# Expert choice in three parts with lists of 512 tokens, two of them worked out beside the experts' products, and the expert bias inside the activation

## The chip, the cores and the metric

The kernel runs on one core of one Trainium2 chip. The metric is the device time of one execution in microseconds (us), and the median of three runs stands for the kernel. A core has five engines with instruction queues of their own: TensorE (PE in the profile), VectorE (DVE), ScalarE (ACT), GpSimd (POOL) and SyncE (SP), which wait for each other on semaphores.

## The reference

Two transformer blocks run one after the other over x of 4 x 1024 tokens of 256 numbers. The change is in the second half of the first block, a mixture of 48 experts in which the experts choose tokens:

```
xf = h.reshape(-1, D)                      # T = 4096 tokens, D = 256
cap = int(1.5 * T / E)                     # E = 48 experts, cap = 128
logits = xf @ Wr.T
vals, idx = top_k(logits.T, cap)           # each expert takes its best 128 tokens
w = softmax(vals)
xg = xf[idx]
h = gelu(einsum('ecd,esdm->ecsm', xg, W1) + b1)      # S = 4 slices, M = 256
y = einsum('ecsm,esmk->ecsk', h, W2) + b2            # K = 64
out = zeros.at[idx].add(y * w)
```

Before it stands an attention of its own, behind it a second block (a Performer with an elu network, and another network); neither is touched.

## The kernel before

The program is a chain of blocks with a barrier between them: `front`, three blocks of `expert_choice`, then `performer` and `networks`. The blocks of `expert_choice` are these.

The first normalises the tokens in 8 groups of 512, writes them to `h_dram`, and puts the logits into `logits`, where rows 0 to 47 hold the first 2048 tokens for each of the 48 experts and rows 64 to 111 the other 2048.

The second block finds the best tokens. VectorE runs 16 rounds over rows of 2048 numbers: `max` gives the 8 largest, `max_index` their places, `match_replace` wipes them out (L825 to L828). Then the two halves of each expert are merged by a few small products and operations, which leaves `index` and `weight` (one column of 128 for each expert). Beside the rounds, SyncE loads the weights of the first 8 experts, and TensorE and ScalarE fold the key and query weights of the second block and work out its constants (`fold_ps`, L899 to L919).

The third block is the loop over the 48 experts. Each expert needs these steps, by the names in the code:

- `gather(e)` on GpSimd: copies the indices to `slot`, then an indirect DMA brings the 128 rows of the expert from `h_dram` to `xg`;
- `turn(e)` on TensorE transposes them, `x_copy(e)` on ScalarE brings them to `xT`;
- `up(e)` on TensorE: 16 products into `h_ps`; VectorE adds the bias (`pre`, L1053), ScalarE applies gelu in one operation of 128 x 1024 (L1027);
- `down(e)` on TensorE: 8 products into `y_ps`; VectorE adds b2 (`biased_y`, L1064);
- `weigh(e)` on ScalarE multiplies by the weights into `y` (L1032), and the scatter of expert e on GpSimd adds the rows to a sum in DRAM by an indirect DMA (L999).

Every engine works its queue in the order that the code gives. TensorE goes up(e + 1), turn(e + 2), down(e). ScalarE goes gelu(e + 1), weigh(e), x_copy(e + 3). GpSimd goes scatter(e), gather(e + LEAD), where `LEAD` is 6, so that six gathers are issued ahead of the first scatter. SyncE loads expert e + 8 once `biased_y` of expert e is there.

Of the kernel before, what the change touches and what calls it, by code (L numbers as in the profile page):

```python
# [12 lines left out]
ALU = mybir.AluOpType  # L13
# [575 lines left out]
TOP = 8  # L589

def expert_choice(nc, mk, g, a):

    HALF = T // 2
    LOW = 64
    ROWS = LOW + E
    with ExitStack() as ctx:
# [6 lines left out]
        weight = t.sb("weight", [P, E])  # L604
        h_dram = nc.dram_tensor("h_dram", (T, D), F32, kind="Internal").ap()
# [10 lines left out]
        with ExitStack() as c2:  # L616
            r = Maker(nc, c2)
            logits = r.sb("logits", [ROWS, HALF])

            with ExitStack() as c3:  # L620
                t = Maker(nc, c3)
                z, hg = t.sb("z", [P, 2, G, D]), t.sb("hg", [P, 2, G, D])
                hT = t.sb("hT", [P, 2, KD, GT])
                wrT = t.sb("wrT", [P, KD, E])
                st, mv, var, rstd, shift = (t.sb("st1", [P, G, 6]), t.sb("mv1", [P, 2, G, 2]), t.sb("var1", [P, 2, G]), t.sb("rstd1", [P, 2, G]),
                                            t.sb("shift1", [P, 2, G]))
                tp, lp, back = t.ps("tp1", [P, 2, KD, GT]), t.ps("lp1", [P, 2, GT]), t.ps("back1", [P, G, D])
                own, blank, var_ready, rstd_ready, shift_ready = (mk.sem("ec_dve"), mk.sem("ec_blank"), mk.sem("ec_var"), mk.sem("ec_rstd"),
                                                                  mk.sem("ec_shift"))
                z_ready, turned, hT_ready, back_done, h_ready = (mk.sem("ec_z"), mk.sem("ec_turned"), mk.sem("ec_hT"), mk.sem("ec_back"),  # L630
                                                                 mk.sem("ec_h"))
                logits_done, logits_out, wrT_done, wrT_copied = (mk.sem("ec_logits"), mk.sem("ec_logits_out"), mk.sem("ec_wrT"),
                                                                 mk.sem("ec_wrT_copied"))
                h_out = [mk.sem("ec_h_out0"), mk.sem("ec_h_out1")]
                part = lambda n: slice(LOW * (n // (NG // 2)), LOW * (n // (NG // 2)) + E)
                with nc.Block() as block:
                    @block.sync
                    def _(sp):
                        for n in range(NG):
                            sp.wait_ge(h_ready, n + 1)  # L640
                            sp.dma_start(h_dram[n * GT:(n + 1) * GT, :].rearrange("(t p) d -> p t d", p=P), hg[:, n % 2]).then_inc(h_out[n % 2], 16)
                        for k in range(2):
                            sp.wait_ge(h_out[k], 16 * (NG // 2))

                    @block.gpsimd
                    def _(pool):
                        pool.memset(logits[32:64, :], LOWEST).then_inc(blank, 1)
                        pool.wait_ge(blank, 1)
                        for n in range(NG):
                            pool.wait_ge(var_ready, n + 1)  # L650
                            if n >= 2:
                                pool.wait_ge(shift_ready, n - 1)
                            rsqrt_rows(pool, rstd[:, n % 2], var[:, n % 2], g.minus_half, G, rstd_ready)

                    @block.vector
                    def _(dve):
                        v = Steps(dve, own)

                        def update(n):
                            for j in range(n * G, (n + 1) * G):  # L660
                                row = g.x[:, j, :]
                                v.mark(dve.scalar_tensor_tensor(row, g.gated[:, n // 2, :], g.tok[:, j:j + 1], row, ALU.mult, ALU.add))
                            v.sync()

                        def statistics(n):
                            if n >= 2:
                                dve.wait_ge(z_ready, n - 1)
                            layer_norm_stats(v, g.spare, st, mv[:, n % 2], var[:, n % 2], G, lambda j: g.x[:, n * G + j, :], LN_EPS, var_ready)

                        def shift_of(n):  # L670
                            dve.wait_ge(rstd_ready, n + 1)
                            dve.scalar_tensor_tensor(shift[:, n % 2], mv[:, n % 2, :, 0], -1.0, rstd[:, n % 2], ALU.mult, ALU.mult).then_inc(shift_ready, 1)

                        def logits_copy(n):
                            dve.wait_ge(logits_done, n + 1)
                            if n == 0:
                                dve.wait_ge(blank, 1)
                            dve.tensor_copy(logits[part(n), n % (NG // 2) * GT:(n % (NG // 2) + 1) * GT], lp[part(n), n % 2, :]).then_inc(logits_out, 1)
# [1714 lines left out]
```

## Time and profile before

| | |
|---|---|
| median of 3 runs | 1726.31 us (1724.62 to 1728.32) |
| profiled execution, its own time | 1728.49 us |
| its span, first to last instruction | 1726.7 us |
| busy: PE, DVE, ACT, POOL | 1495.2, 1171.5, 642.8, 526.5 us |
| block that finds the tokens | about 150 to 270 us |
| loop over the experts | about 270 to 562 us |

### The profile page before, as it was taken

What the parts mean: (1) busy time and instruction counts of PE and PEld (TensorE: products, weight loads), DVE (VectorE), ACT (ScalarE), POOL (GpSimd) and SP (SyncE); (2) the same over time, 40 slices, a digit from 0 to 9 for tenths busy, and PEclk for the clock granted to TensorE, in tenths of its full rate; (3) what the DMA queues carried; (4) which work ended last, traced back from release to release, by engine and by line L of the source; (5) the groups of instructions that cost most, each with busy time, mean ns of one, the idle gap of its engine ahead of it and who ended that gap; (6) DMA issues with size and microseconds to landing.
All of it is one profiled execution on the core that took longest, in us unless ns stands there. A gap on an engine that the chain in (4) does not pass through costs nothing. (4 is left out here: it accounts for less than half of the span.)

```text
span 1726.7 us, 22918 instructions
## 1 busy us (share of the span) xinstructions
PE 1495.2 (87%) x8460; PEld 1248.3 (72%) x8460; DVE 1171.5 (68%) x1867; ACT 642.8 (37%) x947; POOL 526.5 (30%) x511
## 2 busy tenths in 40 slices
PE   8874236999998399999997999999976999989997
PEld 6442236999998266666655788888865888878887
DVE  6576992222222668877737878787856987798886
ACT  1044102333333122222222333333326776766774
POOL 2410003555554012222224200000003555546666
PEclk7788657999999599999998999999997999999999
DMA  5516903999993301112113000000012100000001
GB/s 195 220 37 235 320 6 98 296 292 297 297 291 58 123 25 37 37 37 62 36 49 110 0 25 25 25 25 25 13 52 98 50 25 14 1 1 25 13 25 37
DMA packets 127835, 157.16 MB, mean 91 GB/s; under 512 B 13952, under 2 KB 95992, under 8 KB 126720
## 3 DMA queue, kind: packets, MB, share of 16 engines
q1 hardware_dynamic: 115952, 138.12, 24.6%
q0 software_dynamic: 9216, 12.59, 3.6%
q10 hardware_dynamic: 2576, 5.26, 0.8%
q8 instruction: 54, 0.88, 0.2%
q14 instruction: 37, 0.30, 0.1%
HBM read 122.35 MB, written 33.60 MB: 90 GB/s over the span
## 5 line engine op out<-in xcount | busy, mean ns | idle before, releaser
L2031 POOL TENSOR_TENSOR ff_hid_lo<-ff_hid,ff_hid_hi 128x512 fp32r<-128x512 f32 x128 | 176.0, 1376 | 161.1 <-ACT ff_hid_hi L1940 161.1
L1082 PE MATMUL h_ps<-xT,w 128*128 128x128 f32 x1536 | 192.9, 284 | 1.0 <-ACT xT L1023 1.0
L1082 PEld LDWEIGHTS h_ps<-xT,w 128*128 128x128 f32 x1536 | 186.3, 197 | 1.6 <-issue 0.9
L1053 DVE TENSOR_TENSOR pre<-h_ps,b1T 128x1024 f32<-128x1024 f32 x48 | 58.8, 1225 | 176.4 <-PE h_ps L1082 176.4
L2315 PE MATMUL ff_down<-ff_w_hi,ff_hid_hi 128*128 128x256 f32 x512 | 147.7, 288 | 4.1 <-POOL ff_hid_lo L2031 3.6
L2317 PE MATMUL ff_down<-ff_w_hi,ff_hid_lo 128*128 128x256 f32 x512 | 146.4, 286 | 0.0
L2316 PE MATMUL ff_down<-ff_w_lo,ff_hid_hi 128*128 128x256 f32 x512 | 146.2, 286 | 0.0
L116 POOL TENSOR_TENSOR ff_rstd<-ff_var,minus_half 128x4 f32<-128x4 f32 x24 | 25.5, 1061 | 358.9 <-DVE ff_var L111 356.6
L1117 PE MATMUL k_ring<-w_hi,hT_hi 128*128 128x512 f32 x256 | 118.7, 464 | 9.5 <-DVE hT_lo L1277 6.4
L1458 PE MATMUL k_acc<-wide_rows,hk 128*128 128x512 f32 x256 | 119.7, 599 | 4.3 <-ACT wide_rows L1402 4.3
L1117 PE MATMUL q_ring<-w_hi,hT_hi 128*128 128x512 f32 x256 | 109.8, 429 | 9.8 <-PEq L99 6.8
L1747 PE MATMUL q_out_ps<-kv_sums,wide_rows 128*128 128x256 f32 x512 | 115.5, 379 | 0.0
L2301 PE MATMUL ff_ring<-ff_rowsT_hi,ff_w_hi 128*128 128x512 f32 x256 | 103.0, 402 | 8.4 <-DVE ff_rowsT_lo L2089 3.6
L2315 PEld LDWEIGHTS ff_down<-ff_w_hi,ff_hid_hi 128*128 128x128 f32 x512 | 99.1, 194 | 10.6 <-POOL ff_hid_lo L2031 5.0
L1747 PEld LDWEIGHTS q_out_ps<-kv_sums,wide_rows 128*128 128x128 f32 x512 | 96.3, 190 | 13.2
L2302 PE MATMUL ff_ring<-ff_rowsT_lo,ff_w_hi 128*128 128x512 f32 x256 | 102.4, 400 | 0.0
L2316 PEld LDWEIGHTS ff_down<-ff_w_lo,ff_hid_hi 128*128 128x128 f32 x512 | 99.3, 194 | 4.2
L1119 PE MATMUL k_ring<-w_hi,hT_lo 128*128 128x512 f32 x256 | 102.2, 399 | 0.0
L1118 PE MATMUL k_ring<-w_lo,hT_hi 128*128 128x512 f32 x256 | 101.8, 398 | 0.0
L1119 PE MATMUL q_ring<-w_hi,hT_lo 128*128 128x512 f32 x256 | 101.7, 397 | 0.0
L1118 PE MATMUL q_ring<-w_lo,hT_hi 128*128 128x512 f32 x256 | 101.6, 397 | 0.0
L1393 ACT ACTIVATE k_squares<-k_ring 128x1024 f32<-128x1024 f32 x32 | 32.8, 1025 | 182.3 <-PE k_ring L1119 182.3
(374 smaller groups left out, 3537.4 us busy)
## 6 DMA issues: line engine op xcount, KB each, us to landing
w<-in_L_ffn_W_dram SPq DMA_DIRECT2D x48, 1024.0 KB, 5.8
w<-in_L_ffn_W_dram SPq DMA_DIRECT2D x48, 256.0 KB, 6.1
expert_sum_dram<-f_zero SPq DMA_DIRECT2D x8, 1024.0 KB, 14.9
b_rows<-in_L_ffn_b_dram SPq DMA_DIRECT2D x48, 128.0 KB, 8.8
x<-in_L_attn_x_dram SPq DMA_DIRECT2D x4, 1024.0 KB, 12.4
h_dram<-hg SPq DMA_DIRECT2D x8, 512.0 KB, 2.9
hk<-expert_sum_dram SPq DMA_DIRECT2D x8, 512.0 KB, 4.4
hT_hi<-expert_sum_dram SPq DMA_DIRECT2D x8, 512.0 KB, 5.2
```

The source lines that it names most:

```text
L1082: last = pe.matmul(h_ps[:, q % 2, s * KD + c, :], w1[:, q, s, k, c::KD], xT[:, q % 2, k, :], start=(k == 0), stop=(k == KD - 1))
L1117: pe.matmul(out, x[0], w[0][:, cols], start=start, stop=False)
L1118: pe.matmul(out, x[0], w[1][:, cols], start=False, stop=False)
L1119: return pe.matmul(out, x[1], w[0][:, cols], start=False, stop=stop)
L1458: last = pe.matmul(acc[:, k, cols], hk[:, n % KV_RING, j, k * P:(k + 1) * P], dash[:, n % 2, j, cols], start=(j == 0), stop=(j == G - 1))
L1747: last = pe.matmul(out_ps[:, i % 2, 0:D], qnT[:, i % 2, c, :], kv_out(i // TB)[:, c, :], start=(c == 0), stop=(c == CH - 1))
L2031: pool.tensor_tensor(hid_lo[:, m % PARTS, :], hid[:, m % WHOLES, :], hid_hi[:, m % PARTS, :].bitcast(F32), ALU.subtract).then_inc(part_low, 1)
L2301: pe.matmul(slot(u), high[:, d, cols], x[:, n % 2, d, :], start=(d == 0), stop=False)
L2302: pe.matmul(slot(u), high[:, d, cols], x_low[:, n % 2, d, :], start=False, stop=False)
L2315: pe.matmul(into, hid_hi[:, m % PARTS, tile], high[:, c, :], start=(c == 0 and j % 2 == 0), stop=False)
L2316: pe.matmul(into, hid_hi[:, m % PARTS, tile], low[:, c, :], start=False, stop=False)
L2317: last = pe.matmul(into, hid_lo[:, m % PARTS, tile], high[:, c, :], start=False, stop=(c == CF - 1 and j % 2 == 1))
```

## The change

The experts are dealt with in three parts of 16 (`PHASES`, `EP`). Each part has its own tile of 128 lists, 8 for each of its 16 experts, and each list holds the logits of 512 tokens. SyncE spreads the logits to the lists with three small DMAs for each group. A part needs 16 rounds over rows of 512, and then a merge of the 8 lists of each expert: the lists are sent by TensorE to the 16 experts' rows, sorted down level by level with pairs of max and min until the smallest and the largest of the best 128 are known, each list counts how many of its numbers are above the edge, and the lists' heads are moved to their place by seven steps of doubling length (`move`), once for the indices and once for the weights.

The second and third blocks become one. Part 0 is worked out ahead of the loop. The rounds and the merges of parts 1 and 2 stand in VectorE's queue in slots behind `add(e)`, and TensorE's and ScalarE's pieces of them in slots of the loop. The folds and constants of the second block now use the memory of `h_ps` and of two of the experts' weight buffers, ahead of `up(0)`. The bias of the hidden layer is no longer added by VectorE: gelu reads `h_ps` directly in 8 operations of 128 x 128 with the bias as an operand. `down(e)` also waits for `biased_y` of expert e - 1. `LEAD` is 3: the indices of part 1 come out in the slot of expert 12, and expert 16 is gathered behind the scatter of expert 13. The loops are written out.

```diff
 
 RING = 8
 TOP = 8
+PHASES = 3
+EP = E // PHASES
+LISTS = P // EP
+AHEAD, STARTS, ROUND_SLOTS, COUNTS_AT = 6, (0, 0, 13), (0, 5, 8), (0, 9, 25)
 
...
+                @block.sync
+                def _(sp):
+                    def spread(n):
+                        sp.wait_ge(logits_out, n + 1)
+                        for i in range(PHASES):
+                            sp.dma_start(lists[n * EP:(n + 1) * EP, i, :], stage[i * EP:(i + 1) * EP, n % 2, :]).then_inc(lists_in[n % 2], 16)
+
+                    for n in range(NG):
+                        sp.wait_ge(h_ready, n + 1)
+                        sp.dma_start(h_dram[n * GT:(n + 1) * GT, :].rearrange("(t p) d -> p t d", p=P), hg[:, n % 2]).then_inc(h_out[n % 2], 16)
+                        if n >= 2:
+                            spread(n - 2)
+                    spread(NG - 2)
+                    spread(NG - 1)
...
-            XG, LEAD = 8, 6
+            XG, LEAD = 8, 3
...
+                    def gather(e):
+                        if e % EP == 0:
+                            pool.wait_ge(indexed, e // EP + 1)
+                        if e >= XG:
+                            pool.wait_ge(turned, e - XG + 1)
+                        pool.tensor_copy(slot[:, e % XG], index[:, e:e + 1]).then_inc(slot_set, 1)
                         pool.wait_ge(slot_set, e + 1)
-                        carry_wait(n)
...
+                    def scatter(e):
+                        pool.wait_ge(y_ready, e + 1 + 2)
+                        carry()
+                        pool.indirect_dma_start(out=sums[e % 2], out_offset=bass.IndirectOffsetOnAxis(ap=slot[:, e % XG], axis=0),
+                                                in_=y[:, e % 2, :], in_offset=None, compute_op=ALU.add).then_inc(added[e % 2], 16)
...
+                    for e in range(E):
+                        scatter(e)
+                        if e + LEAD < E:
+                            gather(e + LEAD)
+                        if e:
+                            pool.wait_ge(added[(e - 1) % 2], 16 * ((e + 1) // 2))
+                            pool.sem_inc(y_free, 1)
...
+                    def gelu(e):
+                        act.wait_ge(up_done, e + 1)
+                        for s in range(S):
+                            for c in range(KD):
+                                last = act.activation(act_h[:, e % 2, s * KD + c, :], h_ps[:, e % 2, s * KD + c, :], ACT.Gelu,
+                                                      bias=b1T[:, e * S + s, c:c + 1])
+                        last.then_inc(gelu_done, 1)
...
+                    for e in range(E):
+                        if e + 1 < E:
+                            gelu(e + 1)
+                        weigh(e)
+                        if e + 3 < E:
+                            x_copy(e + 3)
+                        if e == COUNTS_AT[1]:
+                            exps(1)
+                        if e == COUNTS_AT[2]:
+                            exps(2)
...
+                    def rounds(p, first, count):
+                        for n in range(first, first + count):
+                            cols = slice(n * TOP, (n + 1) * TOP)
+                            v(dve.max(top[:, cols], lists[:, p, :]))
+                            v(dve.max_index(at[:, cols], top[:, cols], lists[:, p, :]))
+                            if n < CAP // TOP - 1:
+                                v(dve.match_replace(lists[:, p, :], top[:, cols], lists[:, p, :], LOWEST))
+
+                    def listed(p):
+                        dve.sem_inc(found, 1)
+                        v(dve.tensor_copy(at_f[:], at[:]))
+
...
+                    def sort_steps(lists_left, first, count):
+
+                        for i in range(first, first + count):
+                            j = P >> (i + 1)
+                            of, to = (order[:, (i + x) % 2, 0:lists_left, :].rearrange("e q (b i j) -> e (q b) i j", i=2, j=j) for x in range(2))
+                            v.mark(dve.tensor_tensor(to[:, :, 0, :], of[:, :, 0, :], of[:, :, 1, :], ALU.max))
+                            v.mark(dve.tensor_tensor(to[:, :, 1, :], of[:, :, 0, :], of[:, :, 1, :], ALU.min))
+                            v.sync()
+
+                    def second_level():
...
+                    def move(lists, first, count):
+
+                        for i in range(first, first + count):
+                            of, to, step = lists[:, i % 2, :], lists[:, (i + 1) % 2, :], 1 << i
+                            v(dve.tensor_scalar(to, of, bits[:, 1, i:i + 1], None, ALU.mult))
+                            v(dve.scalar_tensor_tensor(to[:, step:], of[:, 0:P - step], bits[:, 0, i:i + 1], to[:, step:], ALU.mult, ALU.add))
+
...
+                    def add(e):
                         dve.wait_ge(down_done, e + 1)
                         dve.wait_ge(y_ready, e + 1)
-                        dve.tensor_tensor(biased_y[:, q % 2, :], y_ps[:, q % 2, 0:D], b2_rows[:, q, :], ALU.add).then_inc(y_biased, 1)
...
+                    rounds(0, 0, CAP // TOP)
+                    listed(0)
+                    turn_back(0)
+                    first_level(0)
+                    sort_steps(4, 0, 7)
+                    second_level()
+                    sort_steps(2, 0, 7)
+                    last_level()
+                    counts(0)
+                    placed(0)
+                    move(moved, 0, 7)
+                    dve.sem_inc(shifted, 1)
+                    weights_in(0)
+                    indices(0)
+                    move(moved_w, 0, 7)
+                    dve.sem_inc(valued, 1)
+                    rounds(1, 0, AHEAD)
+                    weights(0)
+                    for e in range(E):
+                        add(e)
+                        for p in range(1, PHASES):
+                            k = e - STARTS[p]
+                            if 0 <= k < ROUND_SLOTS[p]:
+                                rounds(p, CAP // TOP - 2 * (ROUND_SLOTS[p] - k), 2)
+                            if k == ROUND_SLOTS[p] - 1:
+                                listed(p)
+                            if e == COUNTS_AT[p] - 4:
...
+                            if e == COUNTS_AT[p] - 1:
+                                sort_steps(2, 0, 7)
+                                last_level()
+                            if e == COUNTS_AT[p]:
+                                counts(p)
+                            if e == COUNTS_AT[p] + 1:
+                                placed(p)
+                                move(moved, 0, 3)
+                            if e == COUNTS_AT[p] + 2:
+                                move(moved, 3, 4)
+                                dve.sem_inc(shifted, 1)
+                            if e == COUNTS_AT[p] + 3:
...
+                    def down(e):
                         pe.wait_ge(gelu_done, e + 1)
+                        if e:
+                            pe.wait_ge(y_biased, e)
...
+                        for k in range(KD):
+                            last = pe.matmul(fold_ps[:, 1024 + c * B:1024 + (c + 1) * B], w_raw[1][:, k, c * P:(c + 1) * P], g.shift_col[:, k, :],
+                                             start=(k == 0), stop=(k == KD - 1))
+                    last.then_inc(wave_consts, 1)
+                    join_weights(0)
+                    turn(0)
+                    pe.wait_ge(consts_out, 1)
+                    up(0)
+                    turn(1)
+                    for e in range(E):
+                        if e + 1 < E:
+                            up(e + 1)
+                        if e + 2 < E:
+                            turn(e + 2)
+                        for p in range(1, PHASES):
...
+                        for p in range(1, PHASES):
+                            if e == COUNTS_AT[p]:
+                                send_edge(p)
         mk.clear_signals()
```

GpSimd's queue where the loop begins, before (L984 with L980 and L987 is a gather, L980 with L999 a scatter; the number of gathers ahead of the first scatter is what to look at):

```order
L984 COPY slot<-index 128x1
L980 TENSOR_TENSOR pool_spare<-minus_half 128x1
L987 DMA xg<-h_dram,slot 128x256
L984 COPY slot<-index 128x1
L980 TENSOR_TENSOR pool_spare<-minus_half 128x1
L987 DMA xg<-h_dram,slot 128x256
L980 TENSOR_TENSOR pool_spare<-minus_half 128x1
L999 DMA expert_sum0_dram<-y,slot 4096x256
L984 COPY slot<-index 128x1
L980 TENSOR_TENSOR pool_spare<-minus_half 128x1
L987 DMA xg<-h_dram,slot 128x256
```

These are the gathers of experts 4 and 5 (four more stand above them), the scatter of expert 0, and the gather of expert 6. The same place in the changed kernel, from the table that the merge needs on:

```order
L882 AFFINE_SELECT before<-same 128x128
L858 COPY slot<-index 128x1
L850 TENSOR_TENSOR pool_spare<-minus_half 128x1
L861 DMA xg<-h_dram,slot 128x256
L858 COPY slot<-index 128x1
L850 TENSOR_TENSOR pool_spare<-minus_half 128x1
L861 DMA xg<-h_dram,slot 128x256
L858 COPY slot<-index 128x1
L850 TENSOR_TENSOR pool_spare<-minus_half 128x1
L861 DMA xg<-h_dram,slot 128x256
L850 TENSOR_TENSOR pool_spare<-minus_half 128x1
L872 DMA expert_sum0_dram<-y,slot 4096x256
```

Only experts 0 to 2 are gathered ahead of the scatter of expert 0; the gather of expert 3 has moved behind it.

TensorE's queue at the start of the loop in the changed kernel (L1182 is `turn`, L1191 `up`, L1202 `down`; the order of the three is that of before):

```order
L1182 MATMUL x_ps<-ident,xg 128x128 x2
L1191 MATMUL h_ps<-xT,w1 128x128 x16
L1182 MATMUL x_ps<-ident,xg 128x128 x2
L1191 MATMUL h_ps<-xT,w1 128x128 x16
L1182 MATMUL x_ps<-ident,xg 128x128 x2
L1202 MATMUL y_ps<-w2,act_h 128x64 x8
L1191 MATMUL h_ps<-xT,w1 128x128 x16
L1182 MATMUL x_ps<-ident,xg 128x128 x2
L1202 MATMUL y_ps<-w2,act_h 128x64 x8
```

These are turn(0), up(0), turn(1), up(1), turn(2), down(0), up(2), turn(3), down(1). Nothing has moved here, so turn(3) stands ahead of down(1).

ScalarE's queue in the loop of the changed kernel (L902 is `x_copy`, L908 gelu, L915 `weigh`):

```order
L902 ACTIVATE xT<-x_ps 128x256
L908 ACTIVATE act_h<-h_ps,b1T 128x128 x8
L915 ACTIVATE y<-biased_y,weight 128x256
L902 ACTIVATE xT<-x_ps 128x256
L908 ACTIVATE act_h<-h_ps,b1T 128x128 x8
```

In the place of one operation of 128 x 1024 from `pre` there are now eight of 128 x 128 from `h_ps`, ahead of each `weigh`.

## Rows read from the trace of the kernel before

**Rows 1.** The page: 40 slices of the span, PE busy and its granted clock.

```profile
PE   8874236999998399999997999999976999989997
PEclk7788657999999599999998999999997999999999
```

**Rows 2.** Windows: window length, each engine's busy us (instructions), PEclk, DMA share, GB/s.

```profile
148.00:270.00 122.00, 35.38 (x189) 32.49 (x189) 113.77 (x94) 8.73 (x10) 0.61 (x3) 0.62 0.53 181
280.00:530.00 250.00, 249.53 (x2159) 249.34 (x2157) 71.61 (x86) 84.97 (x130) 135.04 (x211) 1.00 0.96 275
```

**Rows 3.** Timeline of VectorE, the rounds: start, us, engine, line, operation.

```profile
150.20 2.29 DVE L825 MAX8 top<-logits 112x8 f32<-112x2048 f32 x1 [1.90 <-PEq L636]
...
157.31 2.29 DVE L825 MAX8 top<-logits 112x8 f32<-112x2048 f32 x1
...
259.35 2.29 DVE L826 FIND_INDEX8 at<-top,logits 112x8 uint32<-112x2048 f32 x1
```

**Rows 4.** Groups by line and form, 262 to 290 us: two widths of VectorE.

```profile
L1053 DVE TENSOR_TENSOR pre<-h_ps,b1T 128x1024 f32<-128x1024 f32 x2 | 2.5, 1225 | 15.4 <-PE h_ps L1082 15.4
...
L1064 DVE TENSOR_TENSOR biased_y<-y_ps,b_rows 128x256 f32<-128x256 f32 x1 | 0.4, 425 | 0.6 <-PE y_ps L1091 0.6
```

**Rows 5.** Timeline of TensorE, the constants of the second block.

```profile
215.03 6.96 PE L912 MATMUL fold_ps<-ff_ln_col,w_raw 128*128 128x1 f32 x32 [15.37 <-DMA w_turned<-in_L_attn_W_dram]
221.85 5.08 PE L915 MATMUL fold_ps<-w_turned,ones 128*128 128x256 f32 x16
```

**Rows 6.** Timeline of all engines from the first index to the first gather in the loop.

```profile
270.40 0.19 POOL L984 COPY slot<-index 128x1 uint32<-128x1 uint32 x1 [119.38 <-POOLq L790]
...
274.53 0.70 PE L1073 MATMUL x_ps<-ident,xg 128*128 128x128 f32 x2 [5.64 <-DMA xg<-h_dram,slot]
...
275.27 0.38 ACT L1023 ACTIVATE xT<-x_ps 128x256 f32<-128x256 f32 x1 [7.09 <-PE x_ps L1073]
275.80 5.57 PE L1082 MATMUL h_ps<-xT,w 128*128 128x128 f32 x32 [0.56 <-ACT xT L1023]
...
282.02 1.28 ACT L1027 ACT_TABLE_LOAD   x1
...
288.09 0.42 DVE L1064 TENSOR_TENSOR biased_y<-y_ps,b_rows 128x256 f32<-128x256 f32 x1 [0.60 <-PE y_ps L1091]
288.65 0.51 ACT L1032 ACTIVATE y<-biased_y,weight 128x256 f32<-128x256 f32 x1
...
289.59 1.65 POOL L999 DMA_INDIRECT expert_sum_dram<-y,slot  x1 [0.16 <-POOL pool_spare L980]
...
291.86 1.03 POOL L987 DMA_INDIRECT xg<-h_dram,slot  x1
```

**Rows 7.** Timeline of the loop in its steady state, TensorE and ScalarE of one expert.

```profile
303.27 0.39 PE L1073 MATMUL x_ps<-ident,xg 128*128 128x128 f32 x2
303.50 1.90 PE L1091 MATMUL y_ps<-w,act_h 128*128 128x64 f32 x16
303.70 0.38 ACT L1023 ACTIVATE xT<-x_ps 128x256 f32<-128x256 f32 x1 [2.99 <-PE x_ps L1073]
```

**Rows 8.** Tile xg, issue to landing: the gather at 291.86, at 528.69, all 48.

```profile
DMA to landing us min/median/max: 5.1/5.1/5.1
...
DMA to landing us min/median/max: 2.8/2.8/2.8
...
DMA to landing us min/median/max: 2.8/5.5/7.3
```

**Rows 9.** Timeline: four normalising operations of ScalarE with two operand columns.

```profile
139.82 2.07 ACT L699 ACTIVATE z<-x,shift,rstd 128x256 f32<-128x256 f32 x4
```

**Rows 10.** Timeline of GpSimd where no weights are loaded, and the last scatter.

```profile
526.46 1.60 POOL L999 DMA_INDIRECT expert_sum_dram<-y,slot  x1
...
528.69 1.01 POOL L987 DMA_INDIRECT xg<-h_dram,slot  x1
...
558.26 1.56 POOL L999 DMA_INDIRECT expert_sum_dram<-y,slot  x1 [0.15 <-issue]
```

More of the change, by code:

```diff
@@ L1047, in _, with exps @@
-                    bodies(act, body)
+                        act.activation(y[:, e % 2, :], biased_y[:, e % 2, :], ACT.Copy, scale=weight[:, e:e + 1]).then_inc(y_ready, 1)
+                    def exps(p):
+                        act.wait_ge(edge_ready, p + 1)
+                        act.activation(ex[:], top[:], ACT.Exp, bias=edge[:, 1:2]).then_inc(top_exp, 1)
+                    for k in range(2):
+                        act.dma_start(proj2[:, k, :], a["L1_attn_proj"]).then_inc(proj_in, 16)
@@ new lines, in _ @@
+                    for i, name in enumerate(("Wk", "Wq")):
+                        act.dma_start(w_raw[i], a[f"L1_attn_{name}"].rearrange("(k p) h d -> p k (h d)", p=P)).then_inc(raw_in[i], 16)
+                    act.wait_ge(fold_turned, 1)
+                    act.wait_ge(blank, 1)
+                    for i in range(2):
+                        rows = slice(i * DH, (i + 1) * DH)
+                        last = act.activation(features[rows, i * MF:(i + 1) * MF], fold_ps[rows, 0:MF], ACT.Copy, scale=DN)
@@ L1057, in _ @@
[L1057 to L1061 removed]
+                    v = Steps(dve, own)
+                    def rounds(p, first, count):
[5 more added lines that the diff above has]
+                                v(dve.match_replace(lists[:, p, :], top[:, cols], lists[:, p, :], LOWEST))
@@ new lines, in first_level @@
+                    def first_level(p):
+                        sent = pick_ps[0:EP].rearrange("e h (w i n) -> e h w i n", w=2, i=2)
+                        pair, copy = (order[:, i].rearrange("e (h w) n -> e h w n", w=2) for i in range(2))
+                        dve.wait_ge(lists_sent, p + 1)
+                        v(dve.tensor_copy(copy, sent[:, :, :, 0, :]))
+                        v.mark(dve.tensor_tensor(pair[:, :, 0, :], sent[:, :, 0, 1, :], copy[:, :, 0, :], ALU.max))
+                        v.mark(dve.tensor_tensor(pair[:, :, 1, :], sent[:, :, 1, 1, :], copy[:, :, 1, :], ALU.min))
+                        v.sync()
@@ new lines, in _ @@
+                    for c in range(CF):
+                        last = pe.matmul(fold_ps[:, 512:512 + D], g.ones[:], w_turned[:, c, :], start=(c == 0), stop=(c == CF - 1))
+                    last.then_inc(elu_consts, 1)
+                    send_edge(0)
+                    rank(0)
+                    join_indices(0)
+                    pe.wait_ge(wave_w_in, 16)
+                    for c in range(CF):
+                        for k in range(KD):
+                            last = pe.matmul(fold_ps[:, 1024 + c * B:1024 + (c + 1) * B], w_raw[1][:, k, c * P:(c + 1) * P], g.shift_col[:, k, :],
+                                             start=(k == 0), stop=(k == KD - 1))
```

757 lines of the change are left out of this document (374 added, 383 removed).

## The prediction, written before the changed kernel had run

> **What bounds the kernel now.** I read the page's slices first: TensorE is busy nearly throughout, with a hole in slices 4 to 7 in which its granted clock falls too [rows 1]. The windows then tell two stretches apart [rows 2]. From 148 to 270 us VectorE is busy for 113.8 of 122 us and TensorE for 35.4 at a clock of 0.62: the rounds are the bound. From 280 to 530 us TensorE is busy for 249.5 of 250 us at a clock of 1.00, though the DMA engines are busy for 96% as well: the loop is bound by TensorE. One expert takes 50 products as the records count them, and 2159 in 250 us make 5.79 us for each expert. The timeline shows what starts the loop: the first index is copied at 270.40, its rows have come at 274.53 for turn(0), the first scatter is issued at 289.59 [rows 6], the last at 558.26 [rows 10].
>
> **The rounds.** One takes 157.31 - 150.20 = 7.11 us, and all end at 259.35 + 2.29 = 261.64 [rows 3]. VectorE takes 1225 ns for 1024 columns and 425 for 256 [rows 4], so 1.042 ns a column. Three operations with 1536 columns less save 4.80 us: a round of 512 is 2.31 us, and 16 less one `match_replace` (0.7 us) are 36.3 us instead of 111.4. The lists must land first: the last logits are copied shortly before VectorE's next work at 150.20, behind them stand three small DMAs, and a small transfer takes at least 2.8 us here [rows 8], so I start the rounds at 152.4. They end at 188.7.
>
> **The merge, now longer.** By the same two widths a width of 128 costs 0.29 us, 256 costs 0.43, 512 costs 0.69. A hand-over to TensorE and back is 0.75 us (turn at 274.53, copy at 275.27) and a product at the low clock 0.35 us (16 in 5.57) [rows 6]. So: first turn and two copies 1.4; eight products 3.0; first level 1.6; seven steps of two operations of 256 with their waits 6.3; second level 0.6; seven steps of width 128 4.4; last level 0.9. This puts the edge at 207. It goes out behind TensorE's constants of the second block, which take 6.96 + 5.08 us once two weight matrices have landed [rows 5]. They can be loaded only when both folds are done, about 187, and take about 10 us, so TensorE gets free at about 209.5. Then: hand-over 0.8, counts 1.3, hand-over 0.8, some twelve small operations 3.0, fourteen of width 128 4.2, hand-over 0.8, three small ones 0.8. The indices are there at 221.5. The first slot copy to turn(0) is 4.1 us as before, and turn(0) waits another 0.9 for the product that joins the weights: 226.6 instead of 274.5, 47.9 us earlier. The uncertain part is the load behind the folds; with it 10 us late the gain is 38.
>
> **Up to the first y.** Before, 274.53 to 289.16 (288.65 + 0.51), 14.6 us [rows 6]. VectorE now has fourteen moves of the weights (4.2 us) and six rounds of part 1 (13.9 us) there, beside the first two `up`: it is free at 240.4, and y(0) ends at about 241.3. No further cost.
>
> **The loop: a chain that did not exist.** This is the large term. TensorE's order is up(e + 1), turn(e + 2), down(e). With a lead of 3, the rows for turn(e + 3) are asked for behind the scatter of e, which needs y of e, so down(e). And turn(e + 3) stands ahead of down(e + 1). So each expert's down waits for a whole way round: down, add, weigh, scatter, gather, turn. Before, the lead of 6 put four experts into one such way round, and 5.79 x 4 us covered it. From the landing of rows G(e + 2) the way is:
>
> - turn starts 0.04 later; x_copy 0.43 after turn begins at the high clock [rows 7], 0.74 at the low one [rows 6]; x_copy itself 0.38 and 0.04 to the next;
> - gelu(e + 1) stands in ScalarE's queue ahead of weigh(e), now eight operations. Four of width 256 with operand columns took 2.07 us, with 0.5 us between starts [rows 9]; of width 128 I take 0.36 each, 2.9 us. Bounds: 0.29 and 0.41, 2.3 to 3.3. TensorE's turn, down (1.90) and VectorE's add end earlier at the high clock, and together with it at the low one, so ScalarE sets the time;
> - weigh 0.51 + 0.05, then 0.43 to the scatter's issue (289.16 to 289.59) [rows 6];
> - scatter issued to gather issued 2.27 us (289.59 to 291.86), gather to landing 5.1 us where a fresh load of weights is under way [rows 6, 8]: 7.3 together. Bounds: 2.23 + 2.8 = 5.1 without loads [rows 8, 10], 2.3 + 7.3 = 9.6 at the worst under full load [rows 8]. I take 7.3, as the load of expert e + 8 is issued some 2 us ahead of the scatter each time, but no backlog is left from the last.
>
> The sum is 12.1 us at the high clock, 12.4 at the low one, and I take 12.3. TensorE is then idle for half of each round, and this kernel's trace shows its clock low where it has such gaps: 0.62 at 35.4 busy us of 122 [rows 2]. The Trainium skill, "TensorE: Matmul & The Clock Gate", section on HAM oscillation, says that a loop of short bursts between waits for DMAs can begin each burst at the low clock. The trace of before has no such loop; by this rule the whole sum would be 5 us above mine, at 12.4 a round.
>
> Rows 3 to 47 come this way, so there are 44 rounds from G(3) to G(47): 541 us. G(3) is at 241.3 + 0.43 + 7.3 = 249.0. The exponentials of parts 1 and 2 need another table and gelu's back: two loads of 1.28 us and the operation, 2.9 us, twice [rows 6], on ScalarE and so in the chain: 5.8. After G(47) stand down(45), up(47), down(46), gelu(47), down(47), add and weigh: 13 us. The last scatter is then issued at 809 instead of 558.3: 250.7 us later. Everything behind it is as before.
>
> **What costs nothing.** Rounds and merges of parts 1 and 2 are at most 5.5 us of VectorE in a slot, two rounds (4.6) and an add. In a slot of 12.3 us they are hidden; in a slot of 5.79 they would just fit. The bias that VectorE drops (1.2 us) was not on a path. The wait of down(e) for add(e - 1) is over long before. The loads of experts 6 and 7, now behind the constants, have over 40 us.
>
> **Sum.** 1726.7 - 47.9 + 298.6 (the loop's part of the 250.7) = 1977.4 of span, 1.8 more as a run. The profiled execution of before was 2.2 above the median, so I predict 1977 us, 14.5% slower.
>
> **Rivals.**
> 1. The same chain with queues that are nearly idle at each scatter: 5.1 in the place of 7.3 gives 10.1 a round, 97 us less: 1880. For it speaks that only 1.4 MB is moved in each round of 12 us; against it, the load starts just ahead of the scatter, and the very first scatter of before met just that and took the 7.3. The Trainium skill, "DMA: Bandwidth & Descriptors", on the anatomy of a DMA, gives about 2.0 us fixed and a small part by size; my estimate from that page is 4.5 us for the pair and 9.5 a round, a time of 1854. The trace of before is above that everywhere [rows 8]. Chance 0.13.
> 2. The chain with worse transfers or a GpSimd held up beside VectorE's rounds: 9.6 in the place of 7.3 gives 14.6 and 2078. Under full load the median gather took 5.5 [rows 8], which alone adds only 18 us. Chance 0.10.
> 3. The gathers are hidden after all, and the loop goes on at TensorE's 5.79. Then only the 47.9 us at its head count: 1679, faster. It decides from a round of 5.79 + 47.9 / 44 = 6.9 us downward. The least sum of the rows is 0.04 + 0.43 + 0.42 + 2.3 + 0.56 + 0.43 + 5.1 = 9.3, so the chain would have to be misread. Chance 0.03.
> 4. VectorE falls behind: with 5.5 us in a slot that is never the longest part. No time of its own; 0.01.
>
> **How the numbers follow.** The forecast, a chain at 11.0 to 13.6 us, has 0.73, and its own range is 1920 to 2035. The range 1872 to 2045 takes in the first rival and the lighter half of the second. A measurement of this kernel tells 0.2% from no change. Faster by more than that is the third rival, 0.03; no case ends within 0.2%, 0.01; slower 0.96.
>
> **What would show it.** In the changed trace: rounds of 2.3 us on VectorE ending near 189; turn(0) near 227; TensorE waiting ahead of `x_ps` for the DMA of `xg` for about 6 us at every expert from the third or fourth on, some 250 us in sum, which before happened once (5.64 us, rows 6); 12.3 us from one scatter to the next; a granted clock well under 1.00 in the loop; the last scatter near 809. The prediction is wrong if TensorE never waits there, or if scatter and gather together take other than 5 to 10 us.

## The result, and the profile after

The changed kernel takes 1973.6 us (median of 4 runs, 1967.0 to 1978.0) against 1725.5: 1.144 times as long, 95% interval 1.141 to 1.147. The profiled execution took 1967.02 us with a span of 1965.3. The prediction was 1977.

The page of the changed kernel, its span, TensorE's slices and the DMA engines' (slices are 49 us wide here):

```profile
span 1965.3 us, 23238 instructions
...
PE   8774576677777777389999978999999599998998
...
PEclk7886577777877778699999989999999799999999
DMA  5438444444444542301111040000000310000000
```

Where the loop of before stood as a row of nines for over 200 us [rows 1], there are some eleven slices with TensorE mostly at 60 to 80% and its clock at 0.7 to 0.8, and the DMA engines are down to 40 to 50%. No engine is full. That is how a chain looks, in which each engine waits for the one before it.

Windows of the changed kernel: the loop where weights are loaded, and its last part, where none are (columns as in [rows 2]):

```profile
250.00:500.00 250.00, 178.88 (x1041) 173.66 (x1040) 86.28 (x237) 62.62 (x206) 65.48 (x100) 0.75 0.48 137
...
745.00:790.00 45.00, 36.01 (x255) 35.05 (x255) 2.12 (x5) 14.43 (x50) 15.59 (x25) 0.87 0.18 30
```

1041 products in 250 us are about half of what [rows 2] had in a stretch as long. The waits in the loop, 240 to 800 us:

```profile
POOL pool_spare L850 <- ACT y L915: 391.3, 48, 16.5
...
PE x_ps L1182 <- DMA xg<-h_dram,slot: 146.7, 45, 5.6
...
ACT y L915 <- DVE biased_y L1082: 44.5, 36, 3.0
```

TensorE waits for gathered rows at 45 of 48 experts; before, the trace had this wait at the first one alone [rows 6]. The last row is one that the prediction did not have: ScalarE, with its eight gelu operations done, waits for VectorE's add.

The timeline of one way round, from behind one `turn` to the next:

```profile
399.90 3.65 PE L1202 MATMUL y_ps<-w,act_h 128*128 128x64 f32 x16
400.14 2.17 ACT L908 ACTIVATE act_h<-h_ps,b1T 128x128 f32<-128x128 f32 x8
403.35 6.34 PE L1191 MATMUL h_ps<-xT,w 128*128 128x128 f32 x32
403.60 0.42 DVE L1082 TENSOR_TENSOR biased_y<-y_ps,b_rows 128x256 f32<-128x256 f32 x1 [9.82 <-PE y_ps L1202]
...
404.05 0.51 ACT L915 ACTIVATE y<-biased_y,weight 128x256 f32<-128x256 f32 x1 [1.75 <-DVE biased_y L1082]
...
405.03 1.60 POOL L872 DMA_INDIRECT expert_sum_dram<-y,slot  x1 [0.15 <-POOL pool_spare L850]
...
407.45 1.01 POOL L861 DMA_INDIRECT xg<-h_dram,slot  x1
...
412.48 0.70 PE L1182 MATMUL x_ps<-ident,xg 128*128 128x128 f32 x2 [2.79 <-DMA xg<-h_dram,slot]
412.97 3.51 PE L1202 MATMUL y_ps<-w,act_h 128*128 128x64 f32 x16
```

Read it downward: `down` ends, VectorE adds, ScalarE weighs, GpSimd scatters, GpSimd gathers, and only 5.0 us after that can TensorE run the next `turn` and the next `down`. The `up` that stands between hides most of the wait, but not the chain.

The first gather of the loop (expert 3) is issued at 257.18 and the last (expert 47) at 783.42: 44 rounds, 11.96 us each. Up to the gather at 735.89 a round took 12.3 us (478.7 us for 39), behind it, with no more loads, 9.5 (47.5 for 5). Taken apart, the means of the rounds beside loads are 2.29 us from the issue of a scatter to that of the gather behind it, 4.75 from there to the turn, and 5.22 from the turn to the next scatter; in the rounds without loads they are 2.22, 2.81 and 4.1.

The landing times of `xg`, the gather at 407.45, the gathers from 738 us on, and all 48 (as [rows 8]):

```profile
DMA to landing us min/median/max: 5.0/5.0/5.0
...
DMA to landing us min/median/max: 2.7/2.8/2.8
...
DMA to landing us min/median/max: 2.7/4.7/5.1
```

The head of the loop, first VectorE, then TensorE:

```profile
153.10 0.69 DVE L972 MAX8 top<-lists 128x8 f32<-128x512 f32 x1
...
155.41 0.69 DVE L972 MAX8 top<-lists 128x8 f32<-128x512 f32 x1
...
205.60 0.27 DVE L1016 TENSOR_REDUCE edge_row<-order 16x1 f32<-16x128 f32 x1
222.30 0.16 DVE L1022 COPY edge<-pick_ps 128x1 f32<-128x1 f32 x1 [16.44 <-PE pick_ps L1161]
...
232.16 0.17 DVE L1071 CAST index<-pick_ps 128x16 uint32<-128x16 f32 x1
```

```profile
208.91 6.96 PE L1232 MATMUL h_ps<-ff_ln_col,w 128*128 128x1 f32 x32 [14.97 <-DMA w<-in_L_attn_W_dram]
215.72 6.23 PE L1235 MATMUL h_ps<-w_turned,ones 128*128 128x256 f32 x16
221.88 0.38 PE L1161 MATMUL pick_ps<-edge_row,same 16*128 16x2 f32 x2
...
231.89 6.97 PE L1243 MATMUL h_ps<-ff_shift_col,w 128*128 128x4 f32 x32
...
239.57 0.67 PE L1182 MATMUL x_ps<-ident,xg 128*128 128x128 f32 x2
```

A round of `max`, `max_index` and `match_replace` takes 2.31 us. VectorE has the edge of part 0 (the bound that tells the best 128 of each expert from the rest) ready at 205.9 and then waits 16.4 us for it to come back from TensorE, as the edge's product stands in TensorE's queue behind the constants, whose weights land only at 208.8. A second batch of constants, 6.97 us at 231.89, then stands ahead of turn(0), which comes at 239.57: 35 us earlier than before [rows 6], and 7.1 us after the first copy of an index (232.46) where before it was 4.1.

### The profile page after: what moved, and what is told of

Same layout as the page of the kernel before. It is cut to its first block and busy times, and to the rows that moved or that the text cites. A ratio compares the mean times of both kernels' runs of the same rounds, so it can differ in the third digit from the quotient of the medians.

```text
span 1965.3 us, 23238 instructions
## 1 busy us (share of the span) xinstructions
PE 1627.7 (83%) x8535; PEld 1371.2 (70%) x8535; DVE 1176.3 (60%) x2242; ACT 697.1 (35%) x1289; POOL 529.4 (27%) x512
## 5 line engine op out<-in xcount | busy, mean ns | idle before, releaser
L1082 DVE TENSOR_TENSOR biased_y<-y_ps,b_rows 128x256 f32<-128x256 f32 x48 | 20.4, 425 | 413.3 <-PE y_ps L1202 300.0
L1191 PE MATMUL h_ps<-xT,w 128*128 128x128 f32 x1536 | 252.6, 340 | 1.1 <-ACT xT L902 1.1
L1191 PEld LDWEIGHTS h_ps<-xT,w 128*128 128x128 f32 x1536 | 247.5, 253 | 1.7 <-issue 1.7
L1182 PE MATMUL x_ps<-ident,xg 128*128 128x128 f32 x96 | 26.8, 367 | 146.7 <-DMA xg<-h_dram,slot 146.7
L902 ACT ACTIVATE xT<-x_ps 128x256 f32<-128x256 f32 x48 | 18.4, 383 | 362.2 <-PE x_ps L1182 362.2
L1202 PE MATMUL y_ps<-w,act_h 128*128 128x64 f32 x768 | 138.1, 357 | 0.6 <-ACT act_h L908 0.6
L1202 PEld LDWEIGHTS y_ps<-w,act_h 128*128 128x128 f32 x768 | 135.5, 273 | 1.1 <-ACT act_h L908 0.7
L850 POOL TENSOR_TENSOR pool_spare<-minus_half 128x1 f32<-128x1 f32 x96 | 20.1, 209 | 395.3 <-ACT y L915 391.3
L1182 PEld LDWEIGHTS x_ps<-ident,xg 128*128 128x128 f32 x96 | 15.2, 207 | 155.3 <-DMA xg<-h_dram,slot 155.3
L2479 PEld LDWEIGHTS ff_down<-ff_w_hi,ff_hid_hi 128*128 128x128 f32 x512 | 99.2, 194 | 10.6 <-POOL ff_hid_lo L2195 5.0
L908 ACT ACTIVATE act_h<-h_ps,b1T 128x128 f32<-128x128 f32 x384 | 103.9, 390 | 2.8 <-PE h_ps L1191 2.7
## 6 DMA issues: line engine op xcount, KB each, us to landing
x<-in_L_attn_x_dram SPq DMA_DIRECT2D x4, 1024.0 KB, 12.3
```

Of the source, the lines that this page charges most:

```text
L908: last = act.activation(act_h[:, e % 2, s * KD + c, :], h_ps[:, e % 2, s * KD + c, :], ACT.Gelu, bias=b1T[:, e * S + s, c:c + 1])
L1191: last = pe.matmul(h_ps[:, e % 2, s * KD + c, :], w1[:, e % RING, s, k, c::KD], xT[:, e % 2, k, :], start=(k == 0), stop=(k == KD - 1))
L1202: last = pe.matmul(y_ps[:, e % 2, cols], act_h[:, e % 2, s * KD + c, :], w2[:, e % RING, s, c, :], start=(c == 0), stop=(c == KD - 1))
L2479: pe.matmul(into, hid_hi[:, m % PARTS, tile], high[:, c, :], start=(c == 0 and j % 2 == 0), stop=False)
```

## The experiments

### The lead alone, in the kernel before

```diff
-            XG, LEAD = 8, 6
+            XG, LEAD = 8, 3
```

> The kernel before with one number changed, a lead of 3 gathers in the place of 6. Theory (the loop is a chain from one expert's down through scatter and gather to the next one's turn): about 11.9 us for each of 44 experts in the place of 5.79, 1995 us, between 1960 and 2030. Rival (the loop of the changed kernel is slow because of the rounds and merges beside it, or the eight gelu operations): a lead of 3 alone costs nothing, 1726 us.

Measured: 1989.7 us (1987.0 to 1993.7), ratio 1.154 (1.151 to 1.157). Its waits in the loop:

```profile
PE x_ps L1073 <- DMA xg<-h_dram,slot: 151.7, 46, 5.6
```

One number in the old kernel brings the loss, and the same wait with nearly the same size. A round beside loads takes 12.0 us in this trace, and the loop, from the first scatter to the last, 534.6 us, where before had 268.7 and the changed kernel has 543.2. So the lead alone makes 266 of the 275 us by which the changed loop is longer, and the rounds, the merges and the gelu in eight pieces together come to some 9.

### The gather ahead of the scatter

```diff
                     for e in range(E):
-                        scatter(e)
                         if e + LEAD < E:
                             gather(e + LEAD)
+                        scatter(e)
```

> The changed kernel with the gather of expert e + 3 ahead of the scatter of e, so it waits for the scatter of e - 1 alone. Theory of the chain: two experts share one way round, which is about 12.4 us with the loads at full rate, so 6.2 us for each expert, and 1720 us, between 1700 and 1745. Rival (VectorE's slots of 5.5 us, or POOL held up beside them, slow the loop): 7 us or more for each expert, 1760 us or more. Rival that the order of gather and scatter doesn't matter: 1974.

Measured: 1727.2 us (1721.9 to 1733.0, 10 runs), ratio 1.002 (1.000 to 1.003). The two kinds of transfer have changed places and nothing else, and 246 us are gone. With two experts in one way round an expert takes about half of it, 6.3 us from one scatter to the next (297.6 us for 47), above TensorE's own 5.79: the window from 250 to 500 us shows TensorE nearly full, and a wait for rows is left at 11 of the experts, 11.1 us in all.

```profile
250.00:500.00 250.00, 238.88 (x1975) 235.18 (x1974) 122.97 (x358) 117.10 (x393) 122.93 (x188) 0.97 0.89 256
```

### The gather first and a lead of 4

```diff
-            XG, LEAD = 8, 3
+            XG, LEAD = 8, 4
```

> As the kernel with the gather first, and a lead of 4: three experts share one way round, 4.1 us each, so TensorE's 5.79 us sets the time again. Theory of the chain: 1702 us, between 1690 and 1720, faster than before by what the head of the loop gained (31 us in the trace) less some waits in the slots of the merges. Rival (VectorE falls behind with rounds and merges in slots of 5.79 us): 1720 to 1760.

Measured: 1701.3 us (1699.4 to 1706.3), ratio 0.986 (0.984 to 0.989). Window 280 to 500 us:

```profile
280.00:500.00 220.00, 219.39 (x1889) 217.84 (x1889) 102.42 (x310) 111.84 (x375) 118.38 (x183) 1.00 0.99 285
```

TensorE is full at the high clock, with VectorE's rounds and merges beside it. 1889 products in 220 us, of which a few belong to the merges, are one expert's 50 every 5.82 us. They are not free, though: from the first scatter to the last the loop takes 276.6 us where before had 268.7, and the longest steps, 7.8 and 9.3 us from one scatter to the next, stand at slots of the merges (experts 5, 9, 21 and 25). So the parts beside the loop cost 8 us in all, and the last scatter is 22 us earlier than before, as is the end of the span (1704.6 for 1726.7).

### More work for TensorE while it waits

```diff
                         if e + 1 < E:
                             up(e + 1)
+                        if 1 <= e < E - 2:
+                            pe.wait_ge(gelu_done, e + 1)
+                            for n in range(12):
+                                pe.matmul(h_ps[:, e % 2, 0, :], g.ident[:], g.ident[:], start=True, stop=True)
```

> The changed kernel with 12 products more for each expert while TensorE waits for the gathered rows; they write to a part of h_ps that the next up overwrites, and keep the engine busy. Theory that the low clock lies in the chain (down takes 3.5 us there and 1.9 at the high clock): the granted clock rises to near 1.00 and each round is 1.4 us shorter, 1915 to 1935 us. Rival that ScalarE's queue (x_copy, eight gelu operations, weigh) sets the time from the landing to the scatter, as the prediction had it: 1974, no change beyond 10 us.

The 12 products come once gelu(e + 1) is done and write where the next `up` writes over them.

Measured: 1936.2 us (1932.5 to 1945.5), 37 us less than the changed kernel, just outside the range given. The clock between 250 and 500 us rises from 0.75 to 0.91:

```profile
250.00:500.00 250.00, 218.62 (x1685) 214.38 (x1686) 94.48 (x256) 69.82 (x232) 71.91 (x110) 0.91 0.52 153
```

Many rounds have `down` at 1.90 us, as the first of these two; others still have it slow, as the second:

```profile
401.24 0.50 PE L1182 MATMUL x_ps<-ident,xg 128*128 128x128 f32 x2 [1.83 <-DMA xg<-h_dram,slot]
401.58 1.90 PE L1202 MATMUL y_ps<-w,act_h 128*128 128x64 f32 x16
...
403.57 0.42 DVE L1082 TENSOR_TENSOR biased_y<-y_ps,b_rows 128x256 f32<-128x256 f32 x1 [6.27 <-PE y_ps L1202]
...
413.53 3.06 PE L1202 MATMUL y_ps<-w,act_h 128*128 128x64 f32 x16
```

Work that has no use makes the kernel faster, since the low clock was in the chain: `down` takes 3.5 us there and 1.9 at the high one. The whole gain lies where it should, from the turn to the next scatter: 4.38 us in the mean for 5.22, while the other two parts are as they were (2.27 and 4.74). So in rounds at the low clock ScalarE's queue does not set the time between landing and scatter. At the high clock it is the longer of the two by a hair: in the round of 401.24 the add ends at 403.99 and `weigh` starts at 404.06, straight behind the gelu operations, and turn to scatter is 3.8 us.

### Without the loads

```diff
-                    for e in range(E - RING):
-                        sp.wait_ge(y_biased, e + 1)
-                        load_expert(sp, e + RING, e % RING)
...
-                        pe.wait_ge(w_in[e % RING], 48 * (e // RING + 1))
+                        pe.wait_ge(w_in[e % RING], 48)
```

> The changed kernel without the loads of experts 8 to 47: their products run on the weights of the first eight, so the result is another. It prices the transfer part of the chain. Theory (scatter and gather take longer because the load of an expert's weights is under way): the round falls from 12.2 us where loads run to about 9.3, as between the last gathers of the changed kernel, for some 38 experts: 1865 us, between 1850 and 1885. Rival (the two transfers take the same time without loads, the way round is long for another reason): 1974.

The loads of experts 8 to 47 are left out, so their products run on the weights of the first eight and the output is wrong; the run only prices the transfers.

Measured: 1866.3 us (1863.4 to 1870.8), 107 us less than the changed kernel. The landing of all gathers, and the window of the loop:

```profile
DMA to landing us min/median/max: 2.7/2.8/3.1
...
250.00:500.00 250.00, 196.91 (x1356) 190.94 (x1357) 107.57 (x302) 81.73 (x272) 83.62 (x127) 0.86 0.18 30
```

A round of the same experts takes 9.7 us in this trace, 2.6 less than beside loads. From scatter to gather it is 2.29 as before; from gather to turn 2.85 for 4.75, so 1.9 us are the transfers'; from turn to scatter 4.55 for 5.22, 0.7 us, as the granted clock rises too (0.75 to 0.86 between 250 and 500 us). So about a quarter of the gain is the clock's.

### The expert bias in the activation, alone

```diff
-                        act.wait_ge(biased, e + 1)
-                        act.activation(act_h[:, q % 2], pre[:, q % 2], ACT.Gelu).then_inc(gelu_done, 1)
+                        act.wait_ge(up_done, e + 1)
+                        for s in range(S):
+                            for c in range(KD):
+                                last = act.activation(act_h[:, q % 2, s * KD + c, :], h_ps[:, q % 2, s * KD + c, :], ACT.Gelu,
+                                                      bias=b1T[:, bass.ds(e * S + s, 1), c])
+                        last.then_inc(gelu_done, 1)
...
-                            bias(e + 1, q + 1)
```

> The kernel before with the expert bias in the activation alone: eight gelu operations of 128 x 128 read h_ps, VectorE's bias operation is gone. Theory (hidden behind TensorE's 5.79 us for each expert): 1726 us within 3. Rival (ScalarE's longer queue delays y and shows in the loop): 0.3 us or more for each expert, 1740 or more.

Measured: 1726.0 us (1721.2 to 1731.9), ratio 1.001 (1.000 to 1.002): no difference that can be told. Window 280 to 530 us:

```profile
280.00:530.00 250.00, 249.53 (x2159) 249.34 (x2157) 17.83 (x42) 125.59 (x437) 134.53 (x210) 1.00 0.96 275
```

VectorE falls from 71.6 [rows 2] to 17.8 us, ScalarE rises from 85.0 to 125.6, and TensorE's 249.5 stays.

### The edge ahead of the constants

Made on the kernel with the gather first and a lead of 4.

```diff
                     send_lists(0)
+                    send_edge(0)
+                    rank(0)
                     pe.wait_ge(cols_in, 16 * (3 + 2 * KD + 4))
...
                     last.then_inc(elu_consts, 1)
-                    send_edge(0)
-                    rank(0)
                     join_indices(0)
```

On ScalarE, `exps(0)` moves ahead of the wait for these constants.

> The kernel with the gather first and a lead of 4, and at the head TensorE's two products for the edge and the ranks of part 0 ahead of the constants of the second block, and the exponential ahead of ScalarE's copies of them. Theory (VectorE waits 16.4 us for the edge because it stands behind constants whose weights land late): the indices come 8 to 9 us earlier, 1693 us, between 1688 and 1698. Rival (the constants are needed ahead of up(0) anyway and bound the head): 1701, no change.

Measured: 1690.8 us (1687.4 to 1692.2, 5 runs), ratio 0.980 (0.978 to 0.982), the fastest kernel here. This is 10.5 us under its base (1701.3), for 8 to 9 forecast. TensorE now sends the edge while the weights are still coming in:

```profile
208.00 0.58 PE L1161 MATMUL pick_ps<-edge_row,same 16*128 16x2 f32 x2 [12.03 <-DVEq L1018]
...
211.31 6.96 PE L1234 MATMUL h_ps<-ff_ln_col,w 128*128 128x1 f32 x32 [0.43 <-DMA w<-in_L_attn_W_dram]
...
230.19 0.67 PE L1182 MATMUL x_ps<-ident,xg 128*128 128x128 f32 x2
```

The two profiles show more than the medians, turn(0) at 230.19 for 244.17. Not all of that is the edge's: the folds took 3.8 us each here and 6.7 and 6.6 in the base's profile, as TensorE had the other clock (see the next experiment).

### A load out of the way of the constants' weights

Made on the kernel with the gather first and a lead of 4; SyncE's `dma_start(mod[...])` stands behind the loads of experts 6 and 7.

> The kernel with the gather first and a lead of 4, and the load of 2.5 MB of modulation rows moved behind the loads of experts 6 and 7, out of the time in which the weights for the constants of the second block come in. Theory (those weights land 18 us after their issue because of the transfers ahead of them, and the edge of part 0 waits behind the constants): they land about 7 us earlier and the loop starts some 6 us earlier, 1695 us, between 1691 and 1698. Rival (they are late because they wait for the folds and their write alone): 1701, no change.

> The kernel with the gather first and a lead of 4 once more, on the same chip, as the base of the run beside it: 1701 us within 3.

Measured: 1695.9 us (1695.6 to 1697.2) beside 1704.1 (1697.5 to 1705.8) for its base, so 8 us of gain between the medians, but the base's own runs spread over that much. The time lies in the forecast range, yet little of it comes the way that was forecast. The two matrices took 14.0 and 15.4 us from issue to landing, and 16.9 and 18.6 in the base's profile beside it (16.4 and 18.1 in the changed kernel). That is 3 us, not the 7 that were expected. Nearly all of the rest stands ahead of these loads, in the second fold, here in this run and then in its base:

```profile
185.48 3.84 PE L1222 MATMUL h_ps<-features,w_turned 128*128 128x128 f32 x32 [1.97 <-ACT w_turned L933]
...
185.26 6.52 PE L1222 MATMUL h_ps<-features,w_turned 128*128 128x128 f32 x32 [1.97 <-ACT w_turned L933]
```

The same products took 2.7 us less, at the high clock. The base issues the load of the rows only at 191.79, when its fold is done, so moving that load can't be the reason; other traces of this code have the fold at either length (6.54 in the changed kernel, 3.84 in the one with the gather first). The first scatter is 6.3 us earlier here than in the base's profile (252.9 for 259.2): 3 us for the load, and nearly 3 that come and go with the clock. So other transfers do make these weights late, but this load is a small part of it, and which ones make up the rest was not tried.

## Why the prediction was right

**The chain.** It rests on three statements, that turn(e + 3) stands ahead of down(e + 1), that its rows are asked for behind the scatter of e, and that a lead of 6 had hidden this. The lead alone shows it (1989.7 us), the two swapped lines undo it (1727.2), and a lead of 4 with the swap takes the last of it away (1701.3). The third rival, hidden gathers, is out, and so is the second, transfers of 9.6 us: they took 7.0. VectorE falling behind is out too, as TensorE stays full beside all of VectorE's slots once the chain is gone.

**The size of a round.** Predicted 12.3 us, measured 12.3 while weights are loaded. That is closer than its parts, which were off in opposite directions. From landing to scatter I had 4.8 to 5.1 us; from the turn to the next scatter the trace has 5.2 in the mean, and 5.5 in the round shown (412.48 to 417.97). The term of ScalarE was mis-sized: eight gelu operations take 2.17 us, 0.26 from start to start, where I took 0.36 and 2.9 in all. So at the low clock it was TensorE's `down` (3.5 us) and VectorE's add that set the time, and the clock, which I had counted as 0.3 us a round, costs more: between a round with everything at the high clock (3.8 us from turn to scatter) and one at the low clock (5.5) lie 1.7 us, and the products added as filler took 37 us off, 0.8 a round, though not all rounds had the high clock. The Trainium skill's statement in "TensorE: Matmul & The Clock Gate", on HAM oscillation, that such loops can begin each burst at the low clock, is what this trace shows (3.65, 3.51 and 0.70 us where [rows 7] have 1.90 and 0.39), while I had put the weight of it too low; it isn't so in every round, as some have `down` at 1.90 us here too. From scatter issue to landing I had 7.3, and the trace has 2.42 + 5.0 = 7.4 at 405.03 and 2.29 + 4.75 = 7.0 in the mean up to the turn.

**What the rounds without loads do.** The first rival's condition, idle queues at the scatter, holds for the last rounds, which take 9.5 us instead of 12.3; five of them make 14 us less. With no loads at all the round is 9.7 us, near the 10.1 of this rival. Nothing is loaded behind expert 47, so I should have split the 44 rounds. The last scatter less the first is 543.2 us where I had 567.3, 24 less. Of these 14 are from the last five rounds, 3 lie behind the last gather, which landed in 2.8 us for my 5.1, and 7 in the 39 rounds before, where I had 485.5 us with the table switches and the trace has 478.7. Here the term of the table switches failed, 5.8 us that I added to the chain: they do lengthen the way from turn to scatter (7.0 and 7.1 us), but the gather behind the first of them, issued 6.0 us behind its load's first issue (377.77 and 383.79) where 3.4 us is the usual distance (404.05 and 407.45), landed in 2.8 us instead of 5.0. The two scatter steps there are 13.9 and 10.6 us, 24.5 together, as much as two common rounds. At the second switch they are 14.1 and 9.8, with the gather 4.6 us behind the load and landed in 3.1. The Trainium skill's figure of about 2.0 us fixed for a DMA ("DMA: Bandwidth & Descriptors", anatomy of a DMA) stays below both: a gather alone took 2.8, a scatter that adds 3.8.

**The head.** Here a term failed. I had the indices at 221.5 and turn(0) at 226.6, the trace has 232.2 and 239.6. The step is "they can be loaded only when both folds are done, about 187, and take about 10 us": the first of the two loads needed was issued at 189.9 and the second at 190.6, and they took 16.4 and 18.1 us, beside 2.5 MB of modulation rows and two experts' loads. The edge waited behind them, which makes 11 of the 13 us. The other 2 are a term that I left out: the second batch of constants (6.97 us at 231.89) stands in TensorE's queue ahead of turn(0), where I had only 0.9 us for a product beyond the gather's own 4.1. All else in the merge was right within 2 us: the edge ready at 205.9 for 207, its way to the indices 10 us for 11. Moving the edge ahead gains 10 us, so the order of TensorE's queue is what turned the late load into a late loop. The head gained 35 us in place of 47.9. This error (13 us) and the one in the loop (24 us) go against each other, so the profiled execution came 11 us, not 24, under my sum; it was also the fastest of the four, 6.6 us under their median. That 1977 and 1974 are so near is in part luck.

**TensorE's waits.** I expected some 250 us of them; the trace has 147. The reason is the clock again: `up` takes up to 6.3 us at the low clock and 4.0 at the high one (at 788.35), so TensorE is slow in the time in which it would have waited.

**What costs nothing.** The bias in the activation: 1.001, as said. The rounds and merges in the slots: as said in the changed kernel's long rounds, where the loop is some 9 us longer than with the lead alone. In slots of 5.8 us, where I had that "they would just fit", they cost 8 us in all.

## What to carry to other kernels

A lead over a chain of transfers means that several items share one way round. How many is the lead less what the order of the queues takes off, and the way round divided by that number must stay below the time that the bound engine needs for one item. Here the order takes off 2 with the scatter first and 1 with the gather first, and a way of 12 us shared by 1, 2 and 3 experts gave 12.3, 6.3 and, in place of 4, about the 5.8 of TensorE. When a change makes a number smaller so that something else fits (here the lead, so that the next part's indices are ready), look at the order of the two instructions that the lead counts between before accepting the price; two swapped lines were worth 246 us. A term that is right on the average can be wrong where its condition ends: the last five rounds had no load beside them. And what stands in an in-order queue behind a wait for a load is as late as the load, needed or not.

## What the runs showed of the hardware

- Useless products made the kernel 37 us faster, through the granted clock (0.75 to 0.91).
- The same products of a fold took 6.5 us in one execution and 3.84 in another of the same code ahead of it, with the clock: 2.7 us of difference between two profiles that no edit explains.
- ScalarE's gelu of 128 x 128 with a bias column takes 0.39 us, but eight in a row take 2.17 us, 0.26 from one start to the next.
- A round of `max`, `max_index` and `match_replace` over 512 columns took 2.31 us, as worked out from widths of 256 to 2048 of other operations.
- A gather issued behind a scatter landed 2.8 us after its issue with no weights on the way, and mostly 4.7 to 5.1 us beside a load of 1.4 MB, where the loop's DMA share was only 0.48. Issued 3.4, 4.6 and 6.0 us behind the issue of a load, three of them took 5.0, 3.1 and 2.8. These are gathers of one trace, and no run varied the distance by itself.
